# A graph kernel whose flow layer sorts backward sums into four quarters of 782 columns, and whose node network multiplies those sums as they lie

## The chip, the cores and the metric

The kernel runs on one core of a Trainium2 chip. The time is that of the device, in microseconds (us), from the start of the program to its end; the profile's times are counted from its first instruction. An engine works through its own list of instructions in order and waits for others by semaphores: TensorE (PE, with its weight loads PEld), VectorE (DVE), ScalarE (ACT), GpSimd (POOL), and SyncE (SP), which here only issues transfers.

## The reference

3125 nodes with 32 features, and 53125 edges, sorted by destination, pass through four layers; each adds its result to the nodes, and each starts from the normalised and rectified nodes. They are a relational layer (twice), a sum over neighbours, the flow layer and an attention layer. The change is in the flow layer, with a part of its preparation inside the sum layer:

```python
past, future = (edge_index[0], edge_index[1])
x_past = x[past]
x_future = x[future]
fwd_in = jnp.concatenate([x_future, x_past, edge_attr], axis=1)
flow_fwd = _mlp(fwd_in, W1f, b1f, W2f, b2f)
fwd_agg = jax.ops.segment_sum(flow_fwd, future, num_segments=x.shape[0])
bwd_in = jnp.concatenate([x_past, x_future, edge_attr], axis=1)
flow_bwd = _mlp(bwd_in, W1b, b1b, W2b, b2b)
bwd_agg = jax.ops.segment_sum(flow_bwd, past, num_segments=x.shape[0])
flow_total = jnp.concatenate([fwd_agg, bwd_agg], axis=1)
return _mlp(flow_total, W1n, b1n, W2n, b2n)
```

`_mlp` is a network of two layers with a Relu behind each: 80 inputs, 64 hidden, 32 outputs for an edge; 64, 64, 32 for a node. `past` is the source of an edge, `future` its destination. So every edge gives a forward message, summed at its destination, and a backward message, summed at its source.

## The kernel before

The nodes lie as 25 blocks of 128 (NB = 25, the last with 53). The edges are sorted into T = 440 tiles of 128 edges, each tile with destinations in one block only; their records (16 attributes, a one, destination in the block, source, type) stay in SBUF as `records`. The layers follow each other, each with a block of instructions for every engine; a block ends when all engines are through with theirs.

**Preparation (`flow_front`).** It has three parts that the sum layer runs at the end of its own lists. SP's part (lines 1200 to 1218) loads 16 pieces of weights, the last two, `W2f` and `W2b`, only once VectorE has zeroed `flow_w2` (`w_zero`). VectorE's part (1220 to 1236) clears the buffers and works out, for each edge, where its backward message goes: the source number is split by shifts and masks into q = (source / 128) mod 4 and j = (source / 512) x 128 + source mod 128, so j runs over QJ = 6 x 128 + 53 = 821 values. `source_j` holds j, and `source_q_mask` a one in column q of four. GpSimd's part writes the row of numbers `iota_j`, QJ long.

**The flow loop (`flow_layer`, from line 1240).** It takes four tiles at a time (G = 4), 110 groups, written out five to a round with as many buffers. For a group GpSimd gathers the source rows (1287); VectorE makes one-hots of the destinations (1306); TensorE turns them (1388), picks the destination rows with them (1396) and turns the inputs (1406); ScalarE copies each result out of PSUM (1362, 1370). `first_products` (1412) and `second_products` (1417) are the edge network, with ScalarE's Relu between them (1366). VectorE adds the bias (1324), adds up the picked rows for the next group (1316), takes the Relu and splits the fp32 messages into three bf16 parts (1330 to 1336). Between these steps it makes four one-hots of j, `flow_onehot_j`, 128 x QJ (1311). Last, `flow_by_q` (1341) sets the 32 backward values of each edge into one of four sets of 32 columns, by its q.

`add_up` then makes, for each of 4 tiles and 3 parts, one *triple* of products: a forward one of 32 columns into `flow_acc_fwd`, and two backward ones into `flow_acc_bwd`, whose rows are (q, feature) and whose columns are j:

```python
pe.matmul(accF[:, bass.ds(cols[b, t], F)], hot[b][:, t, :], top(M[b][:])[:, k, t, 0:F],
          start=False, stop=True, skip_group_check=True)
for lo, hi in ((0, BANK), (BANK, QJ)):
    last = pe.matmul(accB[:, lo:hi], S[b][:, t, k, :],
                     J[b][:, t, lo:hi], start=False, stop=True, skip_group_check=True)
```

BANK is 512. TensorE's list is written out by hand (`step`): for each group turn_onehots, first_products of the group before, 3 triples of the group three back, second_products, pick_destinations, 7 triples, turn_inputs, 2 triples.

**The node network (lines 1452 to 1529).** The backward sums lie with features in rows and j in columns; VectorE copies them out (1465), then the forward sums (1466). TensorE turns the backward sums in seven pieces of 128 columns (1504), each of which is four node blocks, and VectorE puts them beside the forward sums in `flow_total`, 128 x 25 x 64 (1471). Only then does `turn` turn `flow_total` block by block (1511, four blocks into one bank), VectorE copies (1478), TensorE multiplies 512 columns by the 64 x 64 weights `node_w1` (1522), ScalarE takes Relu (1489). This pass has seven turns, the last with one block. At the end TensorE makes the 25 output products (1527, each two records) and VectorE adds them to the nodes and normalises. The attention layer follows with transposes of the nodes (519).

## Time and profile before

| | us |
|---|---|
| median of three timed runs | 3510.24 |
| their range | 3508.18 to 3512.7 |
| span of the profiled execution | 4186.2 |
| flow stage in it (first one-hots to the last product) | 2281 to 3108 |
| node network in it (first copy to the last output product) | 3108 to 3142 |

The profiled execution has no time of its own beside its span. In the page's summary TensorE's products are busy for 2723.7 us (65%), VectorE for 2656.6 (63%), GpSimd for 2327.0 (56%), ScalarE for 533.4 (13%), and the mean granted clock of TensorE is 0.746. These are averages over layers with different limits. "busy us, mean ns" of a group are the union of its instructions and the mean of one record; records of products overlap, since the next starts before the one ahead has drained. In a timeline, consecutive instructions of a kind are merged ("x4"), with the start of the first and their common time; the bracket is the engine's idle time ahead of it and what ended it.

### The profile page before, as it was taken

How to read it: one execution, taken by the hardware profiler on the slowest of the kernel's cores; microseconds unless marked ns; L12 is line 12 of the kernel's file. 1: busy time of each engine (PE TensorE's matmuls, PEld its weight loads, DVE VectorE, ACT ScalarE, POOL GpSimd, SP SyncE). 2: the span in 40 equal slices, each digit the busy share in tenths (PEclk: the TensorE clock that was granted, in tenths of full speed). 3: DMA queues.
4: the chain of work that ended last, by engine and by line, in shares of the span. 5: the costliest groups of instructions: out<-in, count | busy, mean ns of one | idle time of the engine just before them, and what ended most of it. 6: DMA issues, size and time to landing. Idle time of an engine off the chain costs nothing. (4 is left out here: it accounts for less than half of the span.)

```text
span 4186.2 us, 55154 instructions
## 1 busy us (share of the span) xinstructions
PE 2723.7 (65%) x18509; PEld 1820.0 (43%) x18619; DVE 2656.6 (63%) x8007; ACT 533.4 (13%) x1242; POOL 2327.0 (56%) x2253
## 2 busy tenths in 40 slices
PE   0221001898895888957886899999994555555551
PEld 0100001676663676735554566666652222222221
DVE  9001002888854888868887688888854666665667
ACT  0000000000010000000100222222211222222220
POOL 3777774666606666446664566666725444444430
PEclk9555555777765777778887899999985667676665
DMA  5111002111111111111111000000000000000010
GB/s 88 39 37 26 7 7 62 21 21 21 19 62 38 21 22 22 13 22 23 24 24 16 10 10 10 11 10 11 11 4 21 16 17 17 17 17 16 18 14 4
DMA packets 125021, 91.49 MB, mean 22 GB/s; under 512 B 59542, under 2 KB 110678, under 8 KB 124118
## 3 DMA queue, kind: packets, MB, share of 16 engines
q0 software_dynamic: 70912, 41.10, 7.4%
q1 hardware_dynamic: 53846, 46.89, 4.7%
q8 instruction: 164, 2.69, 0.3%
q14 instruction: 99, 0.81, 0.1%
HBM read 60.42 MB, written 27.41 MB: 21 GB/s over the span
## 5 line engine op out<-in xcount | busy, mean ns | idle before, releaser
L732 POOL DMA_INDIRECT rel_rows<-message_table,message_indices x640 | 647.7, 1012 | 449.7 <-issue 173.8
L1287 POOL DMA_INDIRECT flow_x<-node_table,src_indices x440 | 524.9, 1193 | 293.4 <-PE p_x_turned L1406 153.7
L1655 POOL DMA_INDIRECT att_kv_rows<-kv_table,att_index x440 | 417.5, 949 | 474.4 <-DVE att_index L1666 342.7
L795 DVE TENSOR_SCALAR rel_source_onehot<-rel_sources,node_numbers 128x384 bf16<-128x384 f16 x2000 | 547.4, 321 | 208.3 <-remote 174.1
L393 POOL DMA_INDIRECT sorted_edges<-stage,sorted_row x416 | 429.6, 1033 | 191.7 <-issue 126.3
L1429 PE MATMUL flow_acc_bwd<-flow_onehot_j,flow_by_q 128*128 128x309 bf16 (+1 forms) x2530 | 516.9, 335 | 7.1 <-issue 0.2
L870 PE MATMUL p_rel_picked<-rel_source_onehot,rel_h_parts 128*96 128x384 bf16 x2000 | 458.4, 400 | 33.7 <-issue 24.6
L1691 DVE TENSOR_REDUCE att_tile_max<-p_att_scores 128x4 f32<-128x512 f32 x440 | 292.2, 688 | 236.6 <-PE p_att_scores L1805 166.9
L1038 POOL DMA_INDIRECT sum_rows<-node_table,src_indices x280 | 277.5, 991 | 220.5 <-issue 75.0
L870 PEld LDWEIGHTS p_rel_picked<-rel_source_onehot,rel_h_parts 128*96 128x96 bf16 x2000 | 309.2, 155 | 176.6 <-issue 33.3
L1073 DVE TENSOR_SCALAR sum_source_onehot<-sum_sources,node_numbers 128x512 bf16<-128x512 f16 x1000 | 309.1, 377 | 24.8 <-remote 24.8
L1803 PE MATMUL p_att_scores<-att_mask,identb 128*128 128x512 bf16 x440 | 235.6, 536 | 131.6 <-ACT att_parts_turned L1739 131.6
L1126 PE MATMUL p_sum_picked<-sum_source_onehot,sum_h_stack 128*96 128x512 bf16 x1000 | 271.5, 435 | 74.0 <-issue 51.6
L782 DVE TENSOR_TENSOR rel_onehot<-p_rel_lanes,dst_in_block 128x128 f32<-128x128 f32 x880 | 256.1, 291 | 15.7 <-issue 15.7
L1805 PE MATMUL p_att_scores<-att_parts_turned,att_pick 96*128 96x512 bf16 x440 | 241.7, 549 | 0.0
L1426 PE MATMUL flow_acc_fwd<-flow_messages,flow_onehot 128*128 128x32 bf16 x1320 | 235.4, 178 | 0.0
L624 PE MATMUL p_message<-w_rel,h_transposed 32*128 32x320 f32 x200 | 113.5, 744 | 186.8 <-issue 183.0
L1126 PEld LDWEIGHTS p_sum_picked<-sum_source_onehot,sum_h_stack 128*96 128x96 bf16 x1000 | 136.8, 141 | 195.2 <-issue 108.1
L601 DVE COPY message_rows<-p_message 128x320 f32<-128x320 f32 x50 | 24.6, 493 | 292.8 <-remote 227.0
L1341 DVE TENSOR_TENSOR flow_by_q<-flow_messages,source_q_mask 128x512 bf16<-128x512 bf16 x330 | 207.6, 684 | 0.0
L844 ACT CAST rel_picked<-p_rel_picked 96x384 bf16<-96x384 f32 x80 | 38.1, 476 | 1285.4 <-remote 851.6
L897 PE MATMUL p_rel_terms<-rel_basis_parts,rel_picked 96*128 96x256 bf16 x720 | 149.5, 378 | 74.4 <-issue 59.7
(287 smaller groups left out, 4502.7 us busy)
## 6 DMA issues: line engine op xcount, KB each, us to landing
message_table<-message_rows SPq DMA_DIRECT2D x50, 320.0 KB, 2.1
rel_rows<-message_table,message_indices POOLq DMA_INDIRECT x640
rel_sources<-source_rows SPq DMA_DIRECT2D x80, 96.0 KB
flow_x<-node_table,src_indices POOLq DMA_INDIRECT x440
att_kv_rows<-kv_table,att_index POOLq DMA_INDIRECT x440
sorted_edges<-stage,sorted_row POOLq DMA_INDIRECT x416
sum_sources<-source_rows SPq DMA_DIRECT2D x40, 128.0 KB
sum_rows<-node_table,src_indices POOLq DMA_INDIRECT x280
```

The source lines that it names most:

```text
L393: pool.indirect_dma_start(out=d["sorted"], out_offset=bass.IndirectOffsetOnAxis(ap=row[:, c:c + 1], axis=0), in_=stage[:, c, :], in_offset ...
L732: pool.indirect_dma_start(out=rows[b][:, t, :], out_offset=None, in_=d["messages"], in_offset=bass.IndirectOffsetOnAxis(ap=s["idx_msg"][:, ...
L782: last = dve.tensor_tensor(hot[b][:, lo:hi, :], lanes[:].unsqueeze(1).to_broadcast([P, hi - lo, P]), s["dstl"][:, g * RG + lo:g * RG + hi] ...
L795: last = dve.tensor_scalar(which[g % 2][:, c, :], srcs[b][:], s["node"][:, c:c + 1], None, ALU.is_equal)
L870: last = pe.matmul(pp[g % 2][0:3 * F, 0:RW], hs[:, c].rearrange("p k f -> p (k f)"), which[g % 2][:, c, :], start=(c == 0), stop=(c == NB ...
L1038: pool.indirect_dma_start(out=rows[b][:, t, :], out_offset=None, in_=d["nodes"], in_offset=bass.IndirectOffsetOnAxis(ap=s["idx_src"][:, g ...
L1073: last = dve.tensor_scalar(which[g % 2][:, c, :], srcs[g % bufs][:], node[:, c:c + 1], None, ALU.is_equal)
L1126: last = pe.matmul(pp[g % 2][0:3 * F, 0:PT * P], hs[:, c].rearrange("p k f -> p (k f)"), which[g % 2][:, c, :], start=(c == 0), stop=(c == ...
L1287: pool.indirect_dma_start(out=X[b][:, t, 0:F], out_offset=None, in_=d["nodes"], in_offset=bass.IndirectOffsetOnAxis(ap=s["idx_src"][:, g * ...
L1429: last = pe.matmul(accB[:, lo:hi], S[b][:, t, k, :], J[b][:, t, lo:hi], start=False, stop=True, skip_group_check=True)
L1655: pool.indirect_dma_start(out=KV[b][:, t, :], out_offset=None, in_=d["kv"], in_offset=bass.IndirectOffsetOnAxis(ap=ibuf[b][:, t:t + 1], ax ...
L1691: dve.tensor_reduce(tm[b][:, 0, t, :], pR[t % PR][:].rearrange("p (h e) -> p h e", h=HEADS), AX_X, ALU.max).then_inc(max_ready, 1)
```

## The change

1. `QJ` becomes (3125 + 3) / 4 = 782. A source n now has q = n div 782 and j = n mod 782; q is counted by three comparisons with 782, 1564 and 2346, and j is n - 782 q. The one-hots of j, `iota_j`, the backward products and `backward_sums` shrink from 821 to 782 columns.
2. The node network no longer turns the backward sums. Quarter q's sums already lie as features x nodes, in rows 32 q to 32 q + 31, so they are a moving operand as they lie. `node_w1_backward` has for each q a matrix of 128 rows, zero but for the 32 rows of that quarter, and the backward half of the hidden layer is added to the same bank by it. `flow_total` and its turned copy hold forward sums alone, 32 wide.
3. The copy of the backward sums goes to ScalarE; VectorE starts with the forward sums. The turns run two ahead of the products instead of one.
4. SP's transfers of the node network's weights (now eight) wait until VectorE has also zeroed the padded weights.

```diff
-QJ = (NB // 4) * P + LAST
+QJ = (N + 3) // 4
...
-        sp.dma_start(f["Wn1"][:], a["L2_gnn_W1n"]).then_inc(w_in, 16)
+        sp.wait_ge(w_zero, 2)
+        sp.dma_start(f["Wn1"][:], a["L2_gnn_W1n"][0:F, :]).then_inc(w_in, 16)
+        for q in range(4):
+            sp.dma_start(f["Wn1b"][q * F:(q + 1) * F, q, :], a["L2_gnn_W1n"][F:2 * F, :]).then_inc(w_in, 16)
...
-        sp.wait_ge(w_zero, 1)
...
         dve.memset(f["W2"][:], 0.0).then_inc(w_zero, 1)
+        dve.memset(f["Wn1b"][:], 0.0).then_inc(w_zero, 1)
...
-        v.done(dve.tensor_copy(si[:], s["rec"][:, :, SRC]))
-        v.done(dve.tensor_scalar(si2[:], si[:], 9, 7, ALU.arith_shift_right, ALU.logical_shift_left))
-        v.done(dve.tensor_copy(sf[:], si2[:]))
-        v.done(dve.tensor_scalar(si2[:], si[:], P - 1, None, ALU.bitwise_and))
-        v.done(dve.tensor_copy(f["srcj"][:], si2[:]))
-        v.done(dve.tensor_tensor(f["srcj"][:], f["srcj"][:], sf[:], ALU.add))
-        v.done(dve.tensor_scalar(si2[:], si[:], 7, None, ALU.arith_shift_right))
-        v.done(dve.tensor_scalar(si2[:], si2[:], 3, None, ALU.bitwise_and))
-        v.done(dve.tensor_copy(sf[:], si2[:]))
+        source = s["rec"][:, :, SRC]
+        v.done(dve.tensor_scalar(sf[0][:], source, float(QJ), None, ALU.is_ge))
+        for i in (1, 2):
+            v.done(dve.scalar_tensor_tensor(out=sf[i][:], in0=source, scalar=float((i + 1) * QJ), in1=sf[i - 1][:],
+                                            op0=ALU.is_ge, op1=ALU.add))
+        dve.scalar_tensor_tensor(out=f["srcj"][:], in0=sf[2][:], scalar=float(-QJ), in1=source,
+                                 op0=ALU.mult, op1=ALU.add)
...
-                    dve.tensor_copy(back[:], accB[:, 0:QJ]).then_inc(b_ready, 1)
-                    v.done(dve.tensor_copy(total[:, :, 0:F], accF[:, 0:NB * F].rearrange("p (b f) -> p b f", f=F)))
-                    for c in range(TURNS):
-                        n = P if c < TURNS - 1 else LAST
-                        q = min(4, NB - 4 * c)
-                        dve.wait_ge(b_turned, c + 1)
-                        dve.tensor_copy(total[0:n, 4 * c:4 * c + q, F:2 * F],
-                                        px[c % 2][0:n, 0:q * F].rearrange("p (b f) -> p b f", f=F)).then_inc(b_taken, 1)
+                    dve.tensor_copy(total[:], accF[:, 0:NB * F].rearrange("p (b f) -> p b f", f=F)).then_inc(f_ready, 1)
...
+                    act.copy(back[:], accB[:, 0:QJ]).then_inc(b_ready, 1)
...
+                        last = pe.matmul(bank, Wn1[:], FT[c % 2][:, 0:n], start=True, stop=True)
+                        for q in range(4):
+                            first, end = max(lo, q * QJ), min(lo + n, (q + 1) * QJ)
+                            if first < end:
+                                last = pe.matmul(bank[:, first - lo:end - lo], Wn1b[:, q, :],
+                                                 back[:, first - q * QJ:end - q * QJ],
+                                                 start=False, stop=True, skip_group_check=True)
+                        last.then_inc(h_done, 1)
+
+                    turn(0)
+                    turn(1)
+                    pe.wait_ge(b_ready, 1)
+                    for c in range(TURNS):
+                        hidden(c)
+                        if c + 2 < TURNS:
+                            turn(c + 2)
```

TensorE's list in the node network, before, from its first instruction to the third turn (`p_node` is the turned piece, `p_node_out` the bank of the hidden layer):

```order
L1504 MATMUL p_node<-ident,backward_sums 128x128 x6
L1504 MATMUL p_node<-ident,backward_sums 53x128
L1511 MATMUL p_node<-ident,flow_total 64x128 x8
L1522 MATMUL p_node_out<-flow_total_turned,node_w 64x512
L1511 MATMUL p_node<-ident,flow_total 64x128 x4
L1522 MATMUL p_node_out<-flow_total_turned,node_w 64x512
L1511 MATMUL p_node<-ident,flow_total 64x128 x4
```

The same place with the change:

```order
L1499 MATMUL p_node<-ident,flow_total 32x128 x8
L1510 MATMUL p_node_out<-flow_total_turned,node_w 64x512
L1514 MATMUL p_node_out<-backward_sums,node_w_backward 64x512
L1499 MATMUL p_node<-ident,flow_total 32x128 x4
L1510 MATMUL p_node_out<-flow_total_turned,node_w 64x512
L1514 MATMUL p_node_out<-backward_sums,node_w_backward 64x270
L1514 MATMUL p_node_out<-backward_sums,node_w_backward 64x242
L1499 MATMUL p_node<-ident,flow_total 32x128 x4
```

The seven transposes of the backward sums are gone, and behind each forward product stands a backward one, in two pieces where a quarter ends inside the bank.

SP's list at the end of the sum layer, the difference in its last transfers (the other lines of the difference only have new line numbers):

```order
-L1211 DMA node_w<-in_L_gnn_W1n 64x64
-L1212 DMA node_b<-in_L_gnn_b1n 64x1
-L1213 DMA node_w<-in_L_gnn_W2n 64x32
-L1214 DMA node_w<-in_L_gnn_b2n 1x32
-L1216 DMA flow_w<-in_L_gnn_W2f 64x32
-L1217 DMA flow_w<-in_L_gnn_W2b 64x32
...
+L1211 DMA node_w<-in_L_gnn_W1n 32x64
+L1213 DMA node_w_backward<-in_L_gnn_W1n 32x64 x4
+L1214 DMA node_b<-in_L_gnn_b1n 64x1
+L1215 DMA node_w<-in_L_gnn_W2n 64x32
+L1216 DMA node_w<-in_L_gnn_b2n 1x32
+L1217 DMA flow_w<-in_L_gnn_W2f 64x32
+L1218 DMA flow_w<-in_L_gnn_W2b 64x32
```

Four transfers that stood ahead of the wait for `w_zero` are now eight, and stand behind it.

## Rows read from the trace of the kernel before

**Rows 1.** The page: the span of the profiled execution.

```profile
span 4186.2 us, 55154 instructions
```

**Rows 2.** Windows, flow loop: length; busy PE, PEld, DVE, ACT, POOL; clock, DMA, GB/s.

```profile
2600.00:2800.00 200.00, 198.24 (x1598) 132.30 (x1625) 163.46 (x449) 53.35 (x113) 132.26 (x112) 1.00 0.07 11
```

**Rows 3.** Groups of TensorE in the loop, 2400 to 3000, by form.

```profile
L1429 PE MATMUL flow_acc_bwd<-flow_onehot_j,flow_by_q 128*128 128x512 bf16 x925 | 347.9, 377 | 0.0
L1429 PE MATMUL flow_acc_bwd<-flow_onehot_j,flow_by_q 128*128 128x309 bf16 x1010 | 298.3, 295 | 5.3
...
L1412 PE MATMUL p_hidden<-flow_x_turned,flow_w 81*128 81x512 f32 x168 | 91.8, 628 | 0.0
```

**Rows 4.** Timeline of two groups of the loop, TensorE, then ScalarE: start us, us.

```profile
2604.13 0.18 PE L1426 MATMUL flow_acc_fwd<-flow_messages,flow_onehot 128*128 128x32 bf16 x1
...
2605.26 0.18 PE L1426 MATMUL flow_acc_fwd<-flow_messages,flow_onehot 128*128 128x32 bf16 x1
...
2606.38 0.60 PE L1406 MATMUL p_x_turned<-ident,flow_x 128*81 128x128 f32 x4
...
2607.80 1.08 PE L1412 MATMUL p_hidden<-flow_x_turned,flow_w 81*128 81x512 f32 x2
2608.71 0.18 PE L1426 MATMUL flow_acc_fwd<-flow_messages,flow_onehot 128*128 128x32 bf16 x1
...
2615.01 1.13 PE L1412 MATMUL p_hidden<-flow_x_turned,flow_w 81*128 81x512 f32 x2
...
2607.02 0.58 ACT L1370 COPY flow_x_turned<-p_x_turned 81x512 f32<-81x512 f32 x1 [4.46 <-PE p_x_turned L1406]
...
2614.37 0.58 ACT L1370 COPY flow_x_turned<-p_x_turned 81x512 f32<-81x512 f32 x1 [4.73 <-PE p_x_turned L1406]
```

**Rows 5.** Timeline of the loop, VectorE's first step of a group.

```profile
2610.87 0.42 DVE L1324 TENSOR_TENSOR flow_messages<-p_hidden,flow_b 128x256 f32<-128x256 f32 x1 [1.16 <-issue]
```

**Rows 6.** Windows of the node network and behind it, columns as in rows 2.

```profile
3107.80:3110.00 2.20, 0.44 (x2) 0.20 (x2) 1.89 (x2) 0.00 (x0) 1.93 (x1) 1.00 0.00 0
3110.00:3112.00 2.00, 1.49 (x5) 0.70 (x5) 1.41 (x7) 0.00 (x0) 1.15 (x1) 0.65 0.00 0
3124.00:3128.00 4.00, 4.00 (x8) 0.83 (x6) 0.70 (x2) 0.68 (x1) 0.00 (x0) 0.50 0.00 0
3136.00:3140.00 4.00, 4.00 (x21) 4.00 (x20) 0.00 (x0) 0.00 (x0) 0.00 (x0) 0.50 0.00 0
3150.00:3160.00 10.00, 8.57 (x47) 5.91 (x47) 5.43 (x11) 0.00 (x0) 8.22 (x10) 0.67 0.01 2
```

**Rows 7.** Timeline of the node network, TensorE and VectorE.

```profile
3108.11 1.01 DVE L1465 COPY backward_sums<-flow_acc_bwd 128x821 f32<-128x821 f32 x1 [8.22 <-PEq L1280]
...
3109.18 0.44 PE L1504 MATMUL p_node<-ident,backward_sums 128*128 128x128 f32 x2 [1.39 <-DVE backward_sums L1465]
...
3112.72 1.92 PE L1511 MATMUL p_node<-ident,flow_total 128*64 128x128 f32 x8 [0.27 <-DVE flow_total L1471]
...
3117.45 1.96 PE L1522 MATMUL p_node_out<-flow_total_turned,node_w 64*64 64x512 f32 x2
...
3119.34 1.06 PE L1511 MATMUL p_node<-ident,flow_total 128*64 128x128 f32 x4
...
3131.35 10.88 PE L1527 MATMUL p_node_out<-node_w,node_hidden 65*128 65x32 f32 x50 [0.60 <-ACT node_hidden L1489]
```

**Rows 8.** Timeline, end of the sum stage: SP's queue, VectorE, TensorE.

```profile
2252.11 0.47 SPq L1216 DMA_DIRECT2D flow_w<-in_L_gnn_W2f  x1
...
2254.43 0.61 DVE L1225 CAST source_int<-records 128x440 int32<-128x440 f32 x1
...
2258.70 4.14 DVE L1235 SCALAR_TENSOR_TENSOR source_q_mask<-source_q,records 128x440 bf16<-128x440 f32 x4
...
2261.23 3.19 PE L1116 MATMUL sum_acc<-sum_rows,sum_onehot 128*128 128x32 f32 x14
```

**Rows 9.** Timeline behind the network: the attention's first transposes on TensorE.

```profile
3150.72 5.08 PE L519 MATMUL p_att_turn<-ident,h_nodes 128*32 128x128 f32 x24 [8.49 <-DVEq L1585]
```

More of the change, by code:

```diff
@@ L1452, in flow_layer @@
         with ExitStack() as st2:
-            FT = [sb(st2, f"flow_total_turned{i}", [2 * F, 4 * P]) for i in range(2)]
+            FT = [sb(st2, f"flow_total_turned{i}", [F, 4 * P]) for i in range(2)]
             HT = sb(st2, "node_hidden", [HID + 1, TURNS * 4 * P])
@@ L1498, in _ @@
                 def _(pe):
-                    pe.wait_ge(b_ready, 1)
-                    for c in range(TURNS):
-                        n = P if c < TURNS - 1 else LAST
-                        if c >= 2:
-                            pe.wait_ge(b_taken, c - 1)
-                        pe.transpose(px[c % 2][0:n, 0:P], back[:, c * P:c * P + n], s["ident"][:]).then_inc(b_turned, 1)
-                    pe.wait_ge(b_taken, TURNS)
+                    pe.wait_ge(f_ready, 1)
                     def turn(c):
@@ L1510, in turn, with hidden @@
                         for b in range(4 * c, min(4 * c + 4, NB)):
-                            last = pe.transpose(px[c % 2][0:2 * F, (b % 4) * P:(b % 4 + 1) * P], total[:, b, :],
+                            last = pe.transpose(px[c % 2][0:F, (b % 4) * P:(b % 4 + 1) * P], total[:, b, :],
                                                 s["ident"][:])
                         last.then_inc(t_turned, 1)
-                    turn(0)
-                    for c in range(TURNS):
-                        if c + 1 < TURNS:
-                            turn(c + 1)
+                    def hidden(c):
+                        lo = 4 * P * c
                         n = min(4, NB - 4 * c) * P
+                        bank = po[0:HID, (c % 2) * BANK:(c % 2) * BANK + n]
                         pe.wait_ge(t_taken, c + 1)
```

25 lines of the change are left out of this document (11 added, 14 removed).

## The prediction

> **What bounds the kernel now.** The page comes first, for the scale: the profiled execution spans 4186.2 us [rows 1]. That is 676 us above the median of the timed runs, 3510.2 us, so I use no share of the span. The change touches three places (the end of the sum stage, the flow loop, the node network); for each I read the stretch itself and carry the difference in us over to the median.
>
> In the flow loop, the windows view shows TensorE busy for 198.24 of 200 us at a granted clock of 1.00, which is 2.4 GHz, with VectorE at 163.46 [rows 2]. The loop stands on TensorE's stream. Its groups in that stretch say what fills it: the backward products of 512 and 309 columns are most of it, and 168 records of the input product, two to each group of four tiles, make 84 groups in 600 us, 7.14 us each [rows 3]. The timeline shows the beat: forward product, 512 columns, 309 columns, one such triple every 1.13 / 3 = 0.377 us (2604.13 to 2605.26) [rows 4]. 853 columns at 2.4 GHz are 0.355 us, so the beat is nearly pure streaming. VectorE comes next, and idles 1.16 us ahead of a group's messages [rows 5].
>
> In the node network TensorE again works nearly without a gap, but at a clock of 0.50, 1.2 GHz [rows 6]. Ahead of it lies a chain: between the start of the copy of the backward sums, 3108.11, and the first turning of the totals, 3112.72, are 4.61 us of copies and seven small transposes [rows 7].
>
> **The loop: 39 columns fewer.** The second backward product shrinks from 309 to 270 columns, 3 times for each of 440 tiles, 1320 times. A column costs (377 - 295) / 203 = 0.404 ns by the mean records of the two shapes [rows 3], and 1/2.4 = 0.417 ns by the clock; 39 of them are 15.8 to 16.3 ns. I take 16: 1320 x 16 = 21.1 us. Of a group's 12 x 16 = 192 ns not all need be gained. Two triples lie between the turning of the inputs and the input product, and cover ScalarE's copy. In one group that copy ends at 2607.02 + 0.58 = 2607.60 and the product starts at 2607.80, with room; in the next it ends at 2614.95 and the product starts at 2615.01, so there the copy ended the wait [rows 4]. In such groups the 32 ns of these two triples come back as waiting. Bounds: none, 0, and all 110 groups, 3.5 us; with one of two neighbours late I take half, 1.7. The other covers are safe: VectorE would have to miss 192 ns out of the 1.16 us that it idles, and its own one-hots get shorter. **Loop: -19.4 us**, bounds -17.4 (15.8 ns, all late) and -21.5.
>
> **The end of the sum stage.** VectorE's preparation loses nine conversions, 2254.43 to 2258.70, 4.3 us, and half of a memset; it gains a memset of the padded weights and four operations on 440 elements, each between 0.61 us (the conversion that reads the records) and 1.03 us (a quarter of the 4.14) [rows 8]: 2.4 to 4.1 us, and some 0.5 for the memset. VectorE so ends between 2 us earlier and 0.3 later. It does not end the stage: it is done at 2262.84, TensorE at 2261.23 + 3.19 = 2264.42. Price 0, hidden by TensorE's last additions. On SP's queue eight weight transfers (five of them the split W1n) now stand behind both memsets, with W2f and W2b behind them: ten issues. At about 0.5 us each, as the 0.47 of W2f [rows 8], from 2252.5 on, the last is issued near 2258 and may take 6 us to land before the stage ends later. Nobody else is queued behind them until the node table is written after the norm. Price 0; without the cover it would be one for one.
>
> **The node network.** I count from the start of the first copy, 3108.11. Before, the output products start 23.24 us later and last 10.88 [rows 7].
> - What goes: the chain. The forward and the backward copy now run side by side on VectorE and ScalarE, and the turning starts 1.07 us in, as the first transposes do now [rows 7], instead of 4.61: 3.5 us.
> - What comes: backward products over 3125 columns through 128 rows (weights padded with zeros), in 10 pieces. The forward products keep their 3200 columns, the transposes their 25 x 128.
>
> Both prices are in the trace, one for each clock. Full: a 512-column fp32 product takes 2608.71 - 2607.80 = 0.91 us, and four transposes 0.60, or some 0.11 each in a row [rows 4]. Half: 3119.34 - 3117.45 = 1.89 us [rows 7], and 5.08 / 24 = 0.21 us a transpose [rows 9].
> At full clock: four transposes (0.60), a copy of 512 columns (0.6 to 0.7, as ScalarE's 0.58) and its wait let the products begin at 2.4 us; 6325 columns are 12.35 x 0.91 = 11.2; the 17 transposes behind them 1.8; waits between turns and the starts of more pieces 1.2, and the last Relu with its waits 0.6 (both estimates, from the 0.07 us by which 1.89 exceeds twice 0.91, and the 0.58). Sum 17.2 against 23.24: -6.0. The 50 output records take 0.218 us each now; a full clock would halve them at most. I let it last for a third of them: -1.8, between 0 and -5. **At full clock: -7.8 us.**
> At half clock: products from 2.9, 12.35 x 1.89 = 23.3, transposes 3.6, waits 0.6, Relu 0.6: 31.0. **At half clock: +7.8 us.**
>
> **Which clock.** Now it is 1.00 up to 3110, 0.65 in the next 2 us and 0.50 from there on, though TensorE hardly pauses [rows 6]. Ahead of the fall it idled 1.39 us and then did seven transposes with waits among them [rows 7]. While the products through 64 rows ran, and the output products, it stayed at 0.50. In the stretch 3150 to 3160 it reads 0.67: it rose there, and what had run were 24 transposes through 128 rows, nearly back to back [rows 6, 9]. In the changed kernel the idle stretch stays at 1.4 us, but eight transposes through 128 rows follow at once; then half of all product columns, and every transpose, go through 128 rows. I take the full clock to survive, or to come back soon.
> Two rules of the Trainium skill bear on this, both in "TensorE: Matmul & The Clock Gate". Part 1 says that sustained matmul activity releases the full clock: by that the changed tail has it (-7.8), but so should the network before, and the trace shows 0.50 there. Part 4 (PE-mode transpose) says that the full clock does not engage for transposes: by that the tail would be the half-clock one (+7.8), but the 0.67 behind the 24 transposes speaks against it.
>
> **The sum.** -19.4 + 0 - 7.8 = -27.2 us: 4186.2 becomes 4159.0 in a profile, and the median 3510.2 - 27.2 = **3483.0 us**. A measurement can tell 0.2%, 7.0 us.
>
> **The rivals.**
> - *Half clock in the network* (0.20): the clock falls behind the loop as now and stays down. -19.4 + 7.8 = -11.6: 3498.6. For it: 0.50 through a busy engine. A fall and a return halfway lies between, near 3491.
> - *The loop gives half* (0.07): waits for ScalarE's copies, or late gathers, take the rest. -9.7 - 7.8: 3492.7. Against: only 32 of 192 ns lie in that cover.
> - *The loop gives more* (0.04): the timed runs have it at 1.2 GHz, where 39 columns are 32.5 ns. -42.9 - 7.8: 3459.5. Against: 1.00 in the profile.
> - *Slower* (0.03): the loop stands on the round through ScalarE's copies and not on columns, so that what is saved turns into waiting. It decides once a copy ends behind the one-hots' transposes in every group, as at 2614.95, and nothing of the other ten triples is gained either. With the network at half clock, 0 + 7.8: 3518.0. Against: a beat of triples without a pause.
> - That the change doesn't do what it says has no share: four quarters of 782 hold 3125 nodes, and the order of instructions has the 270 columns.
>
> **How the numbers follow.** Forecast 0.66, the rest as above. Its own range is 3476 to 3490 (output products 0 to -5, the loop's bounds, 2 us of spread between runs). The range for 8 in 10 takes in the half-clock case with its bounds: 3474 to 3502. Faster by over 0.2%, below 3503.2, are the forecast, nearly all of the half clock and both loop cases: 0.90. Within 0.2%: 0.07. Slower: 0.03.
>
> **What would show it.** A triple every 0.361 us in place of 0.377, a group near 6.96 us, VectorE idle about 1.0 us ahead of the messages. Clock 1.00 well past the loop's end, 512-column fp32 products at 0.91 us, output products 17 us behind the first copy. Wrong: a beat of 0.377; clock 0.50 with 1.89 us products and the output products 31 us in; a sum stage that ends on SP or VectorE; a difference in the attention stage, which nothing here touches.

## The result, and the profile after the change

The changed kernel takes 3480.24 us (median of five runs, 3477.77 to 3481.57), the kernel before 3508.18 us in five runs on the same chip (3504.8 to 3512.7). The ratio is 0.9917, with a 95% interval of 0.9905 to 0.9929: faster by 27.9 us, where 27.2 were forecast and 0.2% (7.0 us) can be told from no change. The forecast of the time held. Two of its terms were each off by some 2 to 4 us, in opposite directions, so that the sum came this close is luck; and the experiments also changed the reason for the second. Ratios leave out runs far above all others of their kernel (4599.84 us once for the kernel before, 4839.55 us once for `rows_32`).

The page of the changed kernel gives the scale. Its profiled execution took 3477.77 us, so this span can be set against the median, as that of [rows 1] could not.

```profile
span 3476.0 us, 55173 instructions
```

**The loop.** A window of 200 us, columns as in [rows 2]: TensorE is as busy as before, 198.18 us against 198.24, at the same clock. It still bounds the loop.

```profile
2200.00:2400.00 200.00, 198.18 (x1659) 135.95 (x1687) 167.26 (x465) 55.15 (x116) 145.59 (x118) 1.00 0.07 11
```

TensorE's groups by form in 600 us of the loop (2050 to 2650), as in [rows 3]:

```profile
L1429 PE MATMUL flow_acc_bwd<-flow_onehot_j,flow_by_q 128*128 128x512 bf16 x962 | 349.5, 376 | 0.0
L1429 PE MATMUL flow_acc_bwd<-flow_onehot_j,flow_by_q 128*128 128x270 bf16 x1048 | 291.3, 278 | 5.5
...
L1412 PE MATMUL p_hidden<-flow_x_turned,flow_w 81*128 81x512 f32 x174 | 93.7, 620 | 0.0
```

The second backward product has 270 columns and a mean of 278 ns, 17 less than the 295 of 309 columns. 174 input products are 87 groups in 600 us, 6.90 us each, where [rows 3] had 84.

The timeline of one group shows the beat (the ScalarE row ahead of it is the input copy):

```profile
2300.60 0.58 ACT L1370 COPY flow_x_turned<-p_x_turned 81x512 f32<-81x512 f32 x1 [4.29 <-PE p_x_turned L1406]
...
2301.34 1.08 PE L1412 MATMUL p_hidden<-flow_x_turned,flow_w 81*128 81x512 f32 x2
...
2304.33 0.18 PE L1426 MATMUL flow_acc_fwd<-flow_messages,flow_onehot 128*128 128x32 bf16 x1
...
2304.36 0.42 DVE L1324 TENSOR_TENSOR flow_messages<-p_hidden,flow_b 128x256 f32<-128x256 f32 x1 [1.14 <-PE p_hidden L1417]
...
2306.49 0.18 PE L1426 MATMUL flow_acc_fwd<-flow_messages,flow_onehot 128*128 128x32 bf16 x1
...
2308.22 1.08 PE L1412 MATMUL p_hidden<-flow_x_turned,flow_w 81*128 81x512 f32 x2
```

From 2304.33 to 2306.49 are six triples, 0.360 us each, where [rows 4] had 0.377. From 2301.34 to 2308.22 is a group, 6.88 us. The copy ends at 2301.18, 0.16 us ahead of the product that needs it: no late copy here. VectorE idles 1.14 us ahead of these messages; over the loop it is 1.11 in the median. [rows 5] has 1.16 for one group, but the mean below shows that the kernel before idled more.

**The end of the sum stage.** SP's queue, VectorE and TensorE, as in [rows 8]:

```profile
1931.42 0.33 SPq L1211 DMA_DIRECT2D node_w<-in_L_gnn_W1n  x1
...
1935.84 0.60 SPq L1218 DMA_DIRECT2D flow_w<-in_L_gnn_W2b  x1
...
1936.76 4.16 DVE L1235 SCALAR_TENSOR_TENSOR source_q_mask<-source_q,records 128x440 bf16<-128x440 f32 x4
...
1940.31 1.74 PE L1116 MATMUL sum_acc<-sum_rows,sum_onehot 128*128 128x32 f32 x14
1942.38 0.99 DVE L983 TENSOR_TENSOR x_nodes<-sum_acc,x_nodes 128x800 f32<-128x800 f32 x1 [1.45 <-PEq L1030]
```

The ten transfers are issued by 1936.44, VectorE's preparation ends at 1940.92, TensorE's last additions at 1942.05, and the next step starts behind TensorE's. The edits here cost nothing.

**The node network.** Windows, columns as in [rows 6]. TensorE keeps 1.00 through all products of the hidden layer; in [rows 6] it had 0.65 after two microseconds. It falls as the output products begin.

```profile
2738.00:2740.00 2.00, 1.57 (x5) 0.38 (x4) 1.09 (x2) 0.00 (x0) 1.15 (x1) 1.00 0.00 0
...
2748.00:2752.00 4.00, 4.00 (x14) 1.24 (x13) 0.96 (x2) 1.36 (x2) 0.00 (x0) 1.00 0.00 0
2752.00:2756.00 4.00, 3.55 (x17) 2.36 (x17) 0.00 (x0) 0.97 (x2) 0.00 (x0) 0.83 0.00 0
2756.00:2760.00 4.00, 4.00 (x20) 4.00 (x21) 0.00 (x0) 0.00 (x0) 0.00 (x0) 0.50 0.00 0
```

The timeline, beside [rows 7]:

```profile
2736.09 0.81 ACT L1479 COPY backward_sums<-flow_acc_bwd 128x782 f32<-128x782 f32 x1 [13.39 <-PEq L1280]
...
2737.16 1.05 PE L1499 MATMUL p_node<-ident,flow_total 128*32 128x128 f32 x8 [1.37 <-DVE flow_total L1465]
...
2738.64 1.04 PE L1510 MATMUL p_node_out<-flow_total_turned,node_w 32*64 32x512 f32 x2 [0.43 <-DVE flow_total_turned L1471]
2739.61 1.07 PE L1514 MATMUL p_node_out<-backward_sums,node_w_backward 128*64 128x512 f32 x2
...
2754.21 10.52 PE L1529 MATMUL p_node_out<-node_w,node_hidden 65*128 65x32 f32 x50 [0.45 <-ACT node_hidden L1483]
```

The output products start 18.12 us behind the first copy, where 17.2 were forecast and 23.24 stood before, and last 10.52 us against 10.88. First copy to last output product: 28.64 us against 34.12. The clock falls 18.5 us behind the first copy, 0.4 us into the output products.

### The profile page after: what moved, and what is told of

Same layout as the page of the kernel before. It is cut to its first block and busy times, and to the rows that moved or that the text cites. A ratio compares the mean times of both kernels' runs of the same rounds, so it can differ in the third digit from the quotient of the medians.

```text
span 3476.0 us, 55173 instructions
## 1 busy us (share of the span) xinstructions
PE 2507.7 (72%) x18522; PEld 1736.9 (50%) x18632; DVE 2620.6 (75%) x7995; ACT 547.8 (16%) x1243; POOL 2312.8 (67%) x2253
## 5 line engine op out<-in xcount | busy, mean ns | idle before, releaser
L1287 POOL DMA_INDIRECT flow_x<-node_table,src_indices x440 | 539.4, 1226 | 227.1 <-issue 104.8
L393 POOL DMA_INDIRECT sorted_edges<-stage,sorted_row x416 | 404.3, 972 | 192.0 <-issue 126.5
L1429 PE MATMUL flow_acc_bwd<-flow_onehot_j,flow_by_q 128*128 128x270 bf16 (+1 forms) x2530 | 493.4, 325 | 7.1 <-issue 0.2
L870 PE MATMUL p_rel_picked<-rel_source_onehot,rel_h_parts 128*96 128x384 bf16 x2000 | 428.5, 383 | 1.0 <-issue 0.7
L870 PEld LDWEIGHTS p_rel_picked<-rel_source_onehot,rel_h_parts 128*96 128x96 bf16 x2000 | 293.6, 148 | 124.6 <-issue 3.8
L1126 PE MATMUL p_sum_picked<-sum_source_onehot,sum_h_stack 128*96 128x512 bf16 x1000 | 248.8, 411 | 36.8 <-DVE sum_source_onehot L1073 36.3
L1805 PE MATMUL p_att_scores<-att_mask,identb 128*128 128x512 bf16 x440 | 198.2, 450 | 67.0 <-ACT att_parts_turned L1741 67.0
L782 DVE TENSOR_TENSOR rel_onehot<-p_rel_lanes,dst_in_block 128x128 f32<-128x128 f32 x880 | 239.8, 273 | 0.0
L1807 PE MATMUL p_att_scores<-att_parts_turned,att_pick 96*128 96x512 bf16 x440 | 201.9, 459 | 0.0
L1426 PEld LDWEIGHTS flow_acc_fwd<-flow_messages,flow_onehot 128*128 128x128 bf16 x1320 | 129.0, 98 | 145.5 <-issue 26.6
```

The source lines that it names most:

```text
L393: pool.indirect_dma_start(out=d["sorted"], out_offset=bass.IndirectOffsetOnAxis(ap=row[:, c:c + 1], axis=0), in_=stage[:, c, :], in_offset ...
L870: last = pe.matmul(pp[g % 2][0:3 * F, 0:RW], hs[:, c].rearrange("p k f -> p (k f)"), which[g % 2][:, c, :], start=(c == 0), stop=(c == NB ...
L1126: last = pe.matmul(pp[g % 2][0:3 * F, 0:PT * P], hs[:, c].rearrange("p k f -> p (k f)"), which[g % 2][:, c, :], start=(c == 0), stop=(c == ...
L1287: pool.indirect_dma_start(out=X[b][:, t, 0:F], out_offset=None, in_=d["nodes"], in_offset=bass.IndirectOffsetOnAxis(ap=s["idx_src"][:, g * ...
L1429: last = pe.matmul(accB[:, lo:hi], S[b][:, t, k, :], J[b][:, t, lo:hi], start=False, stop=True, skip_group_check=True)
```

## Experiments

A median is given with the number of runs, and a ratio is against the kernel before on the same chip. "Network" is the time from the first copy to the end of the output products in the kernel's profile, as above.

### Is the profile of before a fair one?

`before_again` is the kernel before, unchanged. 

> The kernel before, unchanged, for a second profile, since the one shown spans 4186 us where the timed runs take 3510. Theory 'columns': its loop has the same beat of 0.376 us a triple and no late copies of the turned inputs, a group every 7.09 us; its node network runs at half clock, the output products start about 23 us after the first copy. Rival 'late copies': one group in three still has the copy 0.3 us late, a group takes 7.14 us, and a part of what the changed kernel gained is these waits gone. Time as the kernel before, within 0.1%.

Measured: 3509.98 us (10 runs, ratio 1.000, 0.9991 to 1.0009). Its page, and one group of its loop:

```profile
span 3510.0 us, 55154 instructions
```

```profile
2300.82 0.58 ACT L1370 COPY flow_x_turned<-p_x_turned 81x512 f32<-81x512 f32 x1 [4.46 <-PE p_x_turned L1406]
...
2301.60 1.08 PE L1412 MATMUL p_hidden<-flow_x_turned,flow_w 81*128 81x512 f32 x2
...
2308.69 1.08 PE L1412 MATMUL p_hidden<-flow_x_turned,flow_w 81*128 81x512 f32 x2
```

VectorE's groups ahead of the messages in 2400 to 2700, here and then in the changed kernel (behind the second bar: the engine's idle time ahead of them, in us):

```profile
L1324 DVE TENSOR_TENSOR flow_messages<-p_hidden,flow_b 128x256 f32<-128x256 f32 x42 | 17.8, 425 | 55.3 <-PE p_hidden L1417 55.3
...
L1324 DVE TENSOR_TENSOR flow_messages<-p_hidden,flow_b 128x256 f32<-128x256 f32 x44 | 18.7, 424 | 49.0 <-PE p_hidden L1417 49.0
```

A group is 7.09 us, and the copy ends 0.20 us ahead of its product, in this group and in the next. The late copies of [rows 4] belonged to that one execution, which ran 676 us over. From the first backward product on, its copy ended less than 0.1 us ahead of the product in 41 of 106 groups, and from the start of the one-hots' turning to the input product it took 0.250 us in the mean with a median of 0.223. Here the copy is late in none, and mean and median are 0.222. The row on which I took 1.7 us back showed something of that execution and not of the kernel. VectorE idles 55.3 / 42 = 1.32 us ahead of a group's messages here and 49.0 / 44 = 1.11 in the changed kernel. So its margin shrank by 0.21 us, as much as the group did. The loop, from the first to the last backward product, takes 774.8 us here and 750.4 in the changed kernel.

### Columns alone, network alone

`wide_821` is the changed kernel with its products still 821 columns wide; the columns from 782 on hold nothing. 

> The changed kernel, but the one-hots and the second backward product keep 821 and 309 columns; the last 39 are never hit. Theory 'columns': the loop takes 110 x 12 x 16.3 ns = 21 to 23 us more than in the changed kernel, 3502, that is 5 to 7 us under the kernel before, which is the node network's share. Rival 'VectorE or waits': the loop's gain came from the division (aligned rows, no late copies) and not from columns; then the time stays near 3480.

```diff
+QW = 821
-        "iotaj": sb(st, "iota_j", [P, QJ], F16),
+        "iotaj": sb(st, "iota_j", [P, QW], F16),
...
-                            for lo, hi in ((0, BANK), (BANK, QJ)):
+                            for lo, hi in ((0, BANK), (BANK, QW)):
```

Measured: 3506.42 us (12 runs, 3499.29 to 3520.68), ratio 0.999 (0.9981 to 0.9999). The gain of the loop is gone: median of its groups 7.09 us, loop 773.9. What is left to the network is 3.2 us, between 0.4 and 6.7. The profiled execution is the slowest of the twelve, and in it the clock fell and stayed down; windows and timeline of its network:

```profile
2764.30:2766.30 2.00, 0.93 (x8) 0.69 (x8) 1.27 (x2) 0.81 (x1) 2.00 (x1) 1.00 0.00 0
2766.30:2768.30 2.00, 1.57 (x4) 0.19 (x2) 1.00 (x2) 0.00 (x0) 1.07 (x1) 0.68 0.00 0
2768.30:2770.30 2.00, 2.00 (x3) 0.29 (x2) 0.00 (x0) 0.00 (x0) 0.00 (x0) 0.50 0.00 0
...
2788.30:2790.30 2.00, 2.00 (x6) 0.81 (x5) 0.26 (x1) 0.59 (x1) 0.00 (x0) 0.50 0.00 0
```

```profile
2795.25 10.87 PE L1530 MATMUL p_node_out<-node_w,node_hidden 65*128 65x32 f32 x50 [0.45 <-ACT node_hidden L1484]
```

First copy at 2764.30, output products at 2795.25: 30.95 us. That is the half-clock rival of the prediction, 31.0 us, with the same list of instructions in the network that kept the clock in the changed kernel's profile. Its network is 41.82 us, 13.2 more than in the changed kernel's profile.

`old_network` keeps 782 columns in the loop and puts the network of before back. Its pieces of 128 columns no longer match the quarters of 782, so backward sums reach wrong nodes; work and order are those of before. 

> The kernel before with 782 columns and the division alone; the node network turns the backward sums as before, in seven pieces of 128, so that they are added to wrong nodes (the last piece has 14 columns). Theory 'columns': the loop's 22 us are gained, the network's are not: 3485 to 3487, network at half clock, output products 23 us after the first copy. Rival 'network matters more': above 3490.

The edit, against the changed kernel:

```diff
-                    dve.tensor_copy(total[:], accF[:, 0:NB * F].rearrange("p (b f) -> p b f", f=F)).then_inc(f_ready, 1)
+                    dve.tensor_copy(back[:], accB[:, 0:QJ]).then_inc(b_ready, 1)
+                    v.done(dve.tensor_copy(total[:, :, 0:F], accF[:, 0:NB * F].rearrange("p (b f) -> p b f", f=F)))
...
+                        pe.transpose(px[c % 2][0:n, 0:P], back[:, c * P:c * P + n], s["ident"][:]).then_inc(b_turned, 1)
```

Measured: 3484.2 us (6 runs), ratio 0.9926 (0.9912 to 0.9939). The narrower products alone give 26 us of 3509.6 by the ratio (21 to 31), loop 751.9 us; the network is 33.93 us as before, at 0.50 from its fourth microsecond on. Both halves of the change add up: 26 and 3 by these two kernels, 28 together, with intervals of 6 to 10 us on each half.

`narrow_743` takes 39 more columns off the products and leaves out the backward sums of the last 39 nodes of each quarter. 

> The changed kernel with another 39 columns less in the one-hots and the second backward product (743 and 231); the backward sums of the last 39 nodes of each quarter are left out. Theory 'columns': the group goes from 6.88 to 6.67 us, the loop from 750.4 to 727.5, the time to 3457. Rival 'another bound is near' (ScalarE's copy of the turned inputs, VectorE, GpSimd's gathers at 4 x 1.25 us): the group stays above 6.75, the time above 3464.

```diff
+QW = 743
-                            for lo, hi in ((0, BANK), (BANK, QJ)):
+                            for lo, hi in ((0, BANK), (BANK, QW)):
```

Measured: 3462.35 us (4 runs), ratio 0.9863 (0.9848 to 0.9878), 46 us below the kernel before on its chip and so some 18 below the changed kernel. Its groups in the same 600 us:

```profile
L1430 PE MATMUL flow_acc_bwd<-flow_onehot_j,flow_by_q 128*128 128x231 bf16 x1071 | 281.6, 263 | 0.0
...
L1413 PE MATMUL p_hidden<-flow_x_turned,flow_w 81*128 81x512 f32 x180 | 97.0, 620 | 0.0
```

The product falls by 15 ns (278 to 263) where the first 39 columns took 17. The median group is 6.716 us: 0.164 less than 6.880, where the first step took 0.209. Per product these are 13.7 and 17.4 ns for the same 39 columns; the mean of both, 15.5, is near the 16 of the prediction. The input copy still ends 0.13 us ahead of its product (2303.93 + 0.58, product at 2304.64), so that cover isn't what took the rest. Split by stretches of the group (medians over the loop), the twelve triples gave 208 ns in the first step and 178 in the second. The second products, from their start to the picking of rows, took 836 ns at 821 and at 782 columns and 848 at 743. The time lies between the two that were expected for columns alone and for another bound. Why the steps differ stays open.

### What holds the clock in the network

`rows_32` lets each backward product go through the first 32 rows of its weights and of the sums in place of all 128. For quarter 0 these are its weights; for the other three they are zeros, so their sums are left out. 

> The changed kernel, but each backward product of the node network goes through the first 32 rows alone (quarter 0's sums with its 32 rows of weights, for every node), same number of products and columns; the sums of the other quarters are left out. Theory 'rows': it was the 128 rows that kept the clock; now it falls to 0.50 inside the network and the output products start 28 to 32 us after the first copy, 10 to 13 us later than in the changed kernel: 3490 to 3494. Rival 'short idle': the clock stayed because TensorE paused only 1.4 us; then the clock stays at 1.00 through the products and the time is that of the changed kernel, 3480.

```diff
-                                last = pe.matmul(bank[:, first - lo:end - lo], Wn1b[:, q, :],
-                                                 back[:, first - q * QJ:end - q * QJ],
+                                last = pe.matmul(bank[:, first - lo:end - lo], Wn1b[0:F, q, :],
+                                                 back[0:F, first - q * QJ:end - q * QJ],
```

Measured: 3491.07 us (6 runs: five of 3487.1 to 3491.91 and one of 4839.55), ratio 0.995 (0.9937 to 0.9963). With the same columns, the same waits and the same number of instructions it is slower than the changed kernel by the intervals. The windows show the clock held for 8 us, then lost until the end of the network; the output products start 24.3 us in, less late than the 28 to 32 expected, and the network is 35.17 us:

```profile
2742.90:2744.90 2.00, 2.00 (x11) 0.89 (x9) 0.55 (x1) 0.68 (x1) 0.00 (x0) 1.00 0.00 0
2744.90:2746.90 2.00, 2.00 (x4) 0.15 (x3) 0.13 (x1) 0.00 (x0) 0.00 (x0) 0.59 0.03 8
...
2756.90:2758.90 2.00, 2.00 (x3) 0.45 (x2) 0.00 (x0) 0.02 (x1) 0.00 (x0) 0.50 0.00 0
```

While it had the clock, its first two products of 512 columns, both through 32 rows:

```profile
2739.47 1.04 PE L1510 MATMUL p_node_out<-flow_total_turned,node_w 32*64 32x512 f32 x2 [0.43 <-DVE flow_total_turned L1471]
2740.35 1.02 PE L1514 MATMUL p_node_out<-backward_sums,node_w_backward 32*64 32x512 f32 x2
```

One follows the other after 0.88 us.

`before_128` is the kernel before with other rows alone: `node_w1` and the turned totals are padded from 64 rows to 128 with zeros (and the zeros are waited for). 

> The kernel before, whose network's products run through 128 rows instead of 64: the turned totals and the weights are padded with rows of zeros, everything else and the chain ahead of it as before. Theory 'rows bring the clock back': it falls to 0.50 some 3 us after the first copy as before, but rises again during the products; the output products start 15 to 19 us after the first copy instead of 23, the time falls by 4 to 9 us against the kernel before. Rival 'rows only hold the clock, they don't raise it': 23 us, no change.

```diff
-        "Wn1": sb(st, "node_w1", [2 * F, HID]),
+        "Wn1": sb(st, "node_w1", [P, HID]),
...
-            FT = [sb(st2, f"flow_total_turned{i}", [2 * F, 4 * P]) for i in range(2)]
+            FT = [sb(st2, f"flow_total_turned{i}", [P, 4 * P]) for i in range(2)]
```

Measured: 3498.77 us (6 runs), ratio 0.9973 (0.996 to 0.9987): 9.8 us by the medians for rows of zeros, between 5 and 14 by the interval. The clock falls 2.3 us behind the first copy, as in the kernel before (2.5 and 3.7), and comes back 6.8 us later, with the products through 128 rows:

```profile
2762.80:2764.80 2.00, 1.69 (x7) 1.21 (x8) 0.51 (x3) 0.00 (x0) 0.00 (x0) 0.50 0.00 0
...
2766.80:2768.80 2.00, 2.00 (x7) 0.73 (x6) 0.55 (x1) 0.68 (x1) 0.00 (x0) 0.72 0.00 0
2770.80:2772.80 2.00, 2.00 (x10) 0.82 (x10) 0.69 (x1) 1.11 (x2) 0.00 (x0) 1.00 0.00 0
```

```profile
2776.15 9.08 PE L1532 MATMUL p_node_out<-node_w,node_hidden 65*128 65x32 f32 x50 [0.81 <-ACT node_hidden L1491]
```

The network is 26.40 us, less than the 28.64 of the changed kernel (the output products start 17.3 us in), and that with the seven transposes, the copies one behind the other and 6.8 us at half clock in it.

`pad_128` does the same to the changed kernel: its forward products go through 128 rows too. 

> The changed kernel with its forward products through 128 rows as well (padded with zeros, GpSimd clears the rows while the sums are copied). Theory 'rows': where the clock falls it comes back within some us, so that no run is more than 4 us above the fastest; median 3478 to 3480. Rival: the spread stays as in the changed kernel (one run in four 5 us or more above the fastest).

```diff
-        "Wn1": sb(st, "node_w1", [F, HID]),
+        "Wn1": sb(st, "node_w1", [P, HID]),
...
-            FT = [sb(st2, f"flow_total_turned{i}", [F, 4 * P]) for i in range(2)]
+            FT = [sb(st2, f"flow_total_turned{i}", [P, 4 * P]) for i in range(2)]
```

Measured: 3478.01 us (5 runs, 3475.23 to 3479.34), ratio 0.9911 (0.9897 to 0.9924), no different from the changed kernel. Its five runs spread over 4 us, but so do the first five of the changed kernel (the four of `after_again` over 8), so whether the padding narrows the spread isn't shown.

```profile
2743.03 1.04 PE L1515 MATMUL p_node_out<-flow_total_turned,node_w 128*64 128x512 f32 x2 [0.43 <-DVE flow_total_turned L1473]
2743.91 1.02 PE L1519 MATMUL p_node_out<-backward_sums,node_w_backward 128*64 128x512 f32 x2
...
2757.73 9.24 PE L1535 MATMUL p_node_out<-node_w,node_hidden 65*128 65x32 f32 x50 [0.70 <-ACT node_hidden L1485]
```

First copy at 2740.48: output products 17.25 us in, 9.24 us long, network 26.49. A forward product is followed after 0.88 us, where the changed kernel took 0.97 (2738.64 to 2739.61) from its 32 rows to 128. With 32 rows in both, `rows_32` took 0.88 too: what costs is the change between 32 and 128 rows and not the 32. A whole turn took 2.55 us in the changed kernel (2741.15 to 2743.70), 2.41 here (2745.41 to 2747.82) and 2.40 in `rows_32` (2741.84 to 2744.24). The new network, padded and at full clock up to its output products, takes no less time than the old one, padded (26.49 and 26.40 us), which has 6.8 us at half clock in it. What the removed transposes and copies save, the 3125 additional columns cost again: an estimate by the 0.91 us for 512 columns puts them at some 5.6 us.

### Does the clock survive by chance, and can the gap be filled?

`after_again` is the changed kernel. 

> The changed kernel, unchanged, a second profile and more runs. One copy of it with 821 columns showed the clock fall 2.7 us after the first copy and stay at 0.50, with the output products 31.0 us in; its first profile kept 1.00 for 18.5 us, 18.1 us in. Theory 'chance': the same kernel has both; most runs near 3480, some near 3493. Rival 'the 39 columns matter to the clock': all runs of this one stay between 3477 and 3483.

Measured: 3479.4 us (4 runs, 3477.26 to 3485.37), ratio 0.9908 (0.9893 to 0.9922). The profiled execution is the 3485.37, and its clock did what it had not done in the first profile:

```profile
2743.00:2745.00 2.00, 1.58 (x5) 0.32 (x4) 1.08 (x2) 0.00 (x0) 1.15 (x1) 0.82 0.00 0
2745.00:2747.00 2.00, 2.00 (x4) 0.33 (x5) 0.00 (x0) 0.12 (x1) 0.00 (x0) 0.50 0.00 0
2747.00:2749.00 2.00, 2.00 (x7) 0.64 (x6) 0.68 (x1) 0.56 (x1) 0.00 (x0) 0.83 0.00 0
2749.00:2751.00 2.00, 2.00 (x10) 0.77 (x8) 0.61 (x1) 0.68 (x1) 0.00 (x0) 1.00 0.00 0
```

It fell 3.2 us behind the first copy and was back 3.4 us later; network 30.12 us. With `wide_821` there are so three courses of the clock through one and the same list of instructions of the network: kept, lost and back, lost for good. Neither expectation came true: one run lies above 3483, but none near 3493, and of the changed kernel's nine runs none is long enough for the last course.

`busy_gap` lets TensorE run five bf16 products of 512 columns into a bank that nobody reads while it waits for the copies. 

> The changed kernel with five bf16 products of 512 columns, whose result is overwritten, ahead of TensorE's wait for the forward sums, so that it streams through 1.07 us of the 1.4 in which it idled. Theory 'idle decides': the clock never falls before the output products, no run is above 3485, median 3478 to 3480, output products 18 us after the first copy. Rival 'rows or chance': the same spread as the changed kernel, with some runs 10 us later.

```diff
+                    for i in range(5):
+                        pe.matmul(px[1][:], s["identb"][:], iotaj[:].bitcast(BF16)[:, 0:BANK], start=True, stop=True)
                     pe.wait_ge(f_ready, 1)
```

Measured: 3478.7 us (5 runs, 3478.02 to 3485.01), ratio 0.9914 (0.9901 to 0.9926): no different from the changed kernel by the intervals. TensorE idled 0.32 us ahead of the network in place of 1.37, and in its profile the clock was kept, as in the changed kernel's first one, so there was nothing to save there. One run, 3485.01, is as long as the profiled one of `after_again`; why isn't known.

`interleaved` makes the output products of each turn behind the hidden products of the next one, into the bank of the forward sums, in place of all at the end. 

> The changed kernel, but the output products of each turn stand one turn behind its hidden products, in the banks of the forward sums, instead of all at the end. Theory 'clock': they now run at 1.00 among 128-row work, 0.125 us a record instead of 0.21, and the last Relu is hidden: the last output product ends about 24 us after the first copy instead of 28.6, the time falls by 4 to 5 us, to 3475 or 3476. Rival 'they cost the same': the stream's waits for Relu or the weight loads eat it, 28 us, 3480; or they drag the clock down, over 35 us, 3487 or more.

```diff
                             turn(c + 2)
+                        if c == 1:
+                            pe.wait_ge(x_ready, 1)
+                        if c >= 1:
+                            outputs(c - 1)
+                    outputs(TURNS - 1).then_inc(o_done, 1)
```

Measured: 3485.26 us in the median (ratio 0.9932, 0.991 to 0.9953), but the six runs are two sets: 3475.63, 3475.67, 3477.35, and 3493.17, 3495.5, 3496.01. The profiled one is of the fast set; in it the clock is kept up to the last eight of the 50 output records, and eight records take 0.98 us in place of some 1.7:

```profile
2744.77 0.98 PE L1522 MATMUL flow_acc_fwd<-node_w,node_hidden 65*128 65x32 f32 x8
...
2757.00:2759.00 2.00, 2.00 (x14) 1.29 (x12) 0.00 (x0) 0.68 (x1) 0.00 (x0) 1.00 0.00 0
```

Its network is 24.1 us. That the slow set lost the clock is likely by its size, but none of it was profiled.

`both` has the two edits together (the filled gap and the interleaved output products), and `both_again` is the same kernel, for more runs. 

> The two edits before together. Theory: 3474 to 3476 and a narrow spread, no run above 3480, clock 1.00 until the last output product. Rival: no better than the interleaved one alone.

> The kernel with both edits again. Its first profile had the network 5.4 us shorter than that of the changed kernel and the stages ahead of the flow layer 3 to 6 us longer. Theory 'chance ahead of it': now the stages ahead take what they take in the others (first one-hots of the flow loop at 1959 to 1962) and the median is 3473 to 3477. Rival 'it is slower ahead each time': 3480 again.

Measured: `both` 3480.39 us (5 runs, 3478.44 to 3481.5), ratio 0.9912 (0.9899 to 0.9924); `both_again` 3475.06 (5 runs, 3469.98 to 3481.89), ratio 0.9907 (0.9894 to 0.9921). None of ten runs lies near 3495, where three of six did without the filled gap. That the filled gap is what prevents it is likely, but no long run was profiled. Three of `both`'s five lie above 3480, where none was expected. The networks are 23.2 us, 5.4 below the changed kernel's, yet the ratios can't be told from its 0.9917 and 0.9908. A part of the reason lies ahead of the flow layer, where these kernels are the same: VectorE's first one-hots of the flow loop start at 1964.8 us in the profile of `both`, at 1958.9 in that of the changed kernel and at 1957.2 in that of `both_again`, whose profiled execution took 3472.09 us. So stages that neither edit touches vary by as much as the network gained. No version of these beats the changed kernel beyond its interval.

The networks of the profiles side by side (clock counted from the first copy):

| kernel | network, us | clock |
|---|---|---|
| `before_again` | 33.96 | 0.50 from 3.7 us on |
| `old_network` | 33.93 | 0.50 from 3.1 us on |
| changed kernel | 28.64 | 1.00 to 18.5 us |
| `after_again` | 30.12 | 0.50 from 3.2 to 6.6 us, and from 20.2 on |
| `wide_821` | 41.82 | 0.50 from 2.7 us on |
| `rows_32` | 35.17 | 0.50 from 8.3 us on |
| `before_128` | 26.40 | 0.50 from 2.3 to 9.1 us, and from 19.3 on |
| `pad_128` | 26.49 | 1.00 to 19.1 us |
| `busy_gap` | 28.36 | 1.00 to 18.9 us |
| `narrow_743` | 27.98 | 1.00 to 19.3 us |
| `interleaved` | 24.1 | 1.00 to 22.0 us |
| `both` | 23.2 | 1.00 throughout |
| `both_again` | 23.2 | 1.00 throughout |

The old chain of copies and small transposes (`before_again`, `old_network`, `before_128`, and the first profile of the kernel before) lost the clock within 4 us of the first copy in four of four profiles. Without the chain, and with an idle stretch of 1.37 us, two of seven did so (`after_again`, `wide_821`); with the gap filled, none of three. So few profiles are little for a share, but they speak for a part of the chain in the early fall.

## Why the prediction was right

| | forecast | measured |
|---|---|---|
| loop: 39 columns | -21.1 | -23.0 (110 groups x 0.209) |
| loop: waits that come back | +1.7 | 0 |
| end of the sum stage | 0 | 0 |
| network to the output products | -6.0 | -5.1 kept clock (23.24 to 18.12), -3.5 with a dip (19.71) |
| output products | -1.8 | -0.4, -0.5 |
| sum | -27.2 | -28.5 with the clock kept, -27.0 with the dip, by the profiles; -27.9 by the medians |

The result came out within 0.7 us of the forecast because the loop gave 3.6 us more than forecast and the network 2.3 less (3.8 with the dip). The mechanism of the loop was right; this closeness was luck.

- **What bounds the loop** held: a beat of triples that streams columns, 0.360 us for the forecast 0.361. A column cost more than I took, 17.4 ns for 39 in place of 16, and nothing came back as waiting: a group of 6.88 in place of 6.96 us.
- **The step that failed** in the loop is the 1.7 us, taken from one late copy in a profile that ran 676 us over. I had refused that profile's shares for the same reason and then took a copy that ended 60 ns ahead of its product in it for a property of the kernel. The rest, 1.9 us, is the price of a column.
- **VectorE** was to idle about 1.0 us and idles 1.11 in the mean. The fall, 0.21 us, is what was forecast; it started from 1.32 and not from the 1.16 of the one group in [rows 5]. In `narrow_743` the median is 1.02, so the margin is used up as columns go, and VectorE's shorter one-hots (0.43 to 0.42 us each) give little of it back.
- **The end of the sum stage** was read right: TensorE ends it, 1.1 us behind VectorE. SP's ten issues took the 5.0 us that ten at 0.5 make.
- **The network** was priced well at each clock: 17.2 us forecast, 18.12 in the changed kernel and 17.25 in the padded one; 31.0 forecast at half clock, 30.95 in `wide_821`. Mis-sized was the gain of the output products, -1.8 us: the clock falls as they start, at 18.5 us here, so they last 10.52 us. In `pad_128` they start 1.9 us ahead of the fall and last 9.24, 1.6 less than before, which is nearly that term.
- **The reason behind the network's gain was incomplete.** I put 3.5 us on the shorter chain and took the clock as a condition. `before_128` shows the reverse: rows of zeros alone give the old network 9.8 us, and its 26.40 us are below the changed kernel's. With both padded, the rewritten network is no shorter than the old one (26.49 and 26.40). And `rows_32`, the rewritten network without its padded rows, has 35.17. So its gain comes from the clock, which the products through 128 rows keep or win back. The shorter chain has a part in it: in the profiles, the clock fell early with the old chain in four of four and without it in two of ten. The few profiles don't separate the two further.
- **The sign of a rise** was read too favourably. The 0.67 of [rows 6] is an average over 10 us: the clock was back for 3.4 us, and then fell again (windows, columns as in [rows 6]). The first return behind the network lasted 3.4 us in every profile here.

```profile
3154.90:3158.30 3.40, 2.69 (x21) 1.91 (x19) 2.05 (x6) 0.00 (x0) 3.10 (x3) 0.99 0.00 0
3158.30:3170.00 11.70, 8.06 (x39) 7.82 (x38) 5.85 (x17) 0.00 (x0) 7.67 (x8) 0.50 0.17 43
```

- **The clock rival** had 0.20. Its course is that of the profile of `wide_821`, whose network is the changed kernel's; a fall with a return is that of `after_again`. The medians of the changed kernel did not follow it.
- **The rival with a slower end** had its decider at a late copy in every group. The margins of 0.20, 0.16 and 0.13 us at 821, 782 and 743 columns show it nearing by 30 to 40 ns a step, and not reached.

## What to carry to other kernels

Where a stream of products bounds a loop, columns are worth their streaming time, as long as each copy's cover still holds: find the smallest margin and watch it shrink. Behind such a loop look at the granted clock before the instruction count: a matmul with few rows may be worth padding with zeros where the clock was lost (9.8 us in `before_128`; in `pad_128`, whose profile kept it up to the output products as the changed kernel's first one did, the median gained nothing that could be told), and a tail must be judged over several runs, since one profile shows one of its courses. A profile whose span doesn't match the timed runs is no source for small waits either.

## What the runs showed of the hardware

- The clock here followed the rows in use, and not the busy time alone. Through 64 rows, TensorE was busy for 4.00 of 4.00 us at 0.50 [rows 6]; with the same products through 128 rows 1.00 was back 6.8 us after its loss (`before_128`). Rows of zeros did this, so it isn't the values in them. `rows_32` alone wouldn't show it, since three quarters of its backward products also have weights of zeros only. "TensorE: Matmul & The Clock Gate", Part 1, of the Trainium skill lets sustained activity release the clock; the 0.50 through 64 rows is against it as it stands. That the moment of the rise varies from run to run stands there too. The three courses here differ by more than a moment: in one the clock never fell before the output products, in one it came back, in one it did not.
- 128 rows are not sufficient: in `wide_821` 0.50 lasted through 28 us of a busy engine, with half of all columns through 128 rows.
- Changing between products of 32 and of 128 rows costs, 0.14 us a turn of the network: 0.97 us from one 512-column fp32 product to the next, 0.88 where both have 128 and also where both have 32.
- One execution of the unchanged kernel spanned 4186.2 us and another 3510.0, and from the first to the last backward product they took 779 and 775 us. Most of the difference lay ahead of the flow loop (VectorE's first one-hots at 2281 and 1962 us) and behind it (1078 and 746 us to the end).
